# Two flamingo layers with a routed expert stage: one-hots of the routing in bf16 from a table of places, fewer filler matmuls ahead of the last turn, and another order of the last products

## The chip, the cores and the metric

One core of one Trainium2 chip. The time is that of the device in microseconds (us), from one launch of the whole program; lower is better. The engines are TensorE (PE; its weight loads are listed apart as PEld), VectorE (DVE), ScalarE (ACT), GpSimd (POOL) and the DMA queues, of which SyncE (SP) issues most.

## The reference

The input x is 2 x 1024 tokens of 256 values. Four stages add to it in turn:

```
x = x + tanh(g_xattn[0]) * L0_xattn(layernorm(x), ctx)   # one head, 77 keys
x = x + tanh(g_ffn[0])   * L0_ffn(layernorm(x))          # 256 -> 1024 -> 256, piecewise gelu on a grid
x = x + tanh(g_xattn[1]) * L1_xattn(layernorm(x), ctx)   # 16 heads, 77 keys
x = x + tanh(g_ffn[1])   * L1_ffn(layernorm(x))          # 8 experts, two choices per token
```

The last stage is the one that the change is about:

```
scores = softmax(xt @ wg)                 # 2048 tokens, 8 experts
gvals, gidx = top_k(scores, 2); gvals /= sum(gvals)
# for choice 0, then choice 1: pos = how many choices of this expert came before
keep = pos < 512                          # room of an expert
disp[expert, pos] = token                 # the tokens gathered by expert
y = gelu(disp @ w1 + b1) @ w2 + b2        # per expert
out[token] += gvals * keep * y[expert, pos]
```

## The kernel before, in words

The 2048 tokens lie in SBUF as 16 tiles of 128. All matmuls of float32 values are split into three (high by high, high by low, low by high part; `split_mm`, lines 1397 to 1402). Each engine has a program of its own, in which its order is written out by hand; engines wait for each other through semaphores. What the change touches lies in three places.

**The end of the second attention.** The tokens go through layer norm, a turn on TensorE and the routing logits in pieces (`PIECES`, line 27): three of four tiles, then two of two tiles. The last piece is round `round_of(3, 4)`. For it VectorE takes the statistics (`last_stats`, line 1229), GpSimd takes a power (`power`, line 577), VectorE scales the rows into `xn` (`apply`, line 951), TensorE turns them (`transpose_x`, line 1418), ScalarE copies the high part (`x_hi`, line 673), VectorE makes the low part (`x_lo`, line 959), and TensorE forms the logits (`logits_columns`, `logits_rows`). On VectorE stand between `apply` and `x_lo` of this piece: `take_logits(2)`, `take_logits(3)` and `top_two(3)` (lines 1175 to 1192). On TensorE stand in front of the turn the filler matmuls `keep_warm(5, 8)` (line 1444; 128 x 512 columns of ones each, whose results nobody reads), and behind it `keep_warm(5, 5)`.

**The routing.** With the two best experts of each token in `ixf` and their marks in `mask_bf`, three matmuls and a scan count the place of each choice within its expert (lines 1260 to 1264). A token's choice, one of 32 (`q`: 2 choices by 16 tiles) per partition, goes to slot 128 a + b, where a (0 to 31, `al`) is a tile of slots and b (0 to 127, `bl`) a row in it. `onehotA` (line 1284, float32) marks a, `onehotB` (line 1279, bf16, made in four parts by `rows_hot`) marks b. Both lie choice by choice, so the compare of one choice against the row `iota_a` or `iota_b` has the choice's own number repeated along the innermost dimension. ScalarE makes `sel_tok` from `onehotA`, multiplied by the partition's number plus one (line 892) and by the tile's number (line 895, 16 instructions). TensorE then sums 32 products of `onehotB[:, q, :]` (the stationary operand) and `sel_tok[:, q, :, :]` (line 1818), which gives each slot its token. VectorE turns that into indices (lines 1295 to 1301), GpSimd gathers the rows (line 636), and TensorE, after 16 fillers, turns the first of them. The gates of the slots follow in the experts' stage: `gate_selection` (line 1322) multiplies `onehotA` by three bf16 parts of the gates, and `gates_of_slots` (line 1826) takes 32 products of `onehotB` and `sel_gate`.

**The experts' stage and its end.** For 10 blocks of 4 pairs TensorE alternates `hidden` of one pair and `project` of the pair three before (`LAG`). The last block holds the tiles 2 and 3 of the last expert. `project` runs over tiles, six matmuls each, for one pair at a time. After tile 2 of the last pair it raises `half_done`, on which VectorE adds the bias (line 1352) and scales by the gate (line 1356), and GpSimd scatters the tile's 128 rows with an add (line 648). Tile 3 follows in the same way on `hT_used`; its sum lies in a PSUM bank of its own (`O_last`).

GpSimd's program in the region: the constants of the routing at lines 609 to 615, among them `iota_a` and `iota_b`, in the shadow of the attention; then low parts of weights (line 583) and powers; the last power (line 625) is followed by nothing until the gathers.

Of the kernel before, what the change touches and what calls it, by code (L numbers as in the profile page):

```python
# [14 lines left out]
P = 128  # L15
# [20 lines left out]
def flamingo_gated_two_layers(nc, x, ctx_512, g_xattn, g_ffn,  # L36
# [32 lines left out]
    with ExitStack() as ctx:  # L69
# [316 lines left out]
        def round_of(stage, c):  # L386
            return ROUNDS.index((stage, c))
# [154 lines left out]
        def _(pool):  # L542
# [68 lines left out]
            pool.iota(iota_a, pattern=[[P, 32]], base=0, channel_multiplier=0, **flag).then_inc(rt_consts, 1)  # L611
            pool.iota(iota_b, pattern=[[1, P]], base=0, channel_multiplier=0, **flag).then_inc(rt_consts, 1)
# [12 lines left out]
            power(round_of(3, 4))  # L625

# [35 lines left out]
        def _(act):  # L662
# [227 lines left out]
            act.wait_ge(rt_consts, 5)  # L890
# [25 lines left out]
        def _(dve):  # L916
# [260 lines left out]
            def top_two(c):  # L1177
# [11 lines left out]
                if c == 0:  # L1189
                    dve.wait_ge(rt_consts, 5)  # L1190
# [76 lines left out]
            mark(dve.tensor_scalar(expert_base, posk, float(CAP), 2.0 * NE * CAP, ALU.is_ge, ALU.mult))  # L1267
            link(dve.tensor_scalar(al.bitcast(I32), posk, 1.0 / P, -(0.5 - 0.5 / P), ALU.mult, ALU.add))
            link(dve.scalar_tensor_tensor(out=expert_base, in0=ixf.rearrange("p k t -> p (k t)"), scalar=float(CAP),
# [3 lines left out]
            link(dve.scalar_tensor_tensor(out=al, in0=al.bitcast(I32), scalar=float(P), in1=expert_base, op0=ALU.mult,  # L1273
                                          op1=ALU.add))
# [121 lines left out]
        def _(pe):  # L1396
# [438 lines left out]
            for G in range(NG + LAG):  # L1835
# [8 lines left out]
                if G >= LAG:  # L1844
                    project(NB_PAIRS + G - LAG)
# [25 lines left out]
```

## Time and profile before

| | us |
|---|---|
| median of 3 runs | 536.08 |
| lowest and highest | 533.62, 538.42 |
| the profiled execution | 534.69 |
| its span, first to last instruction | 533.0 |
| mean granted TensorE clock | 0.966 of full |

The profiled execution is 1.69 us longer than its span. A clock of 1.00 is 2.4 GHz, one of 0.50 is 1.2 GHz. Starts in the trace count from the start of the span. "Idle before" in brackets is the idle time of the engine ahead of the row, with what ended it; a row with "x4" merges four instructions.

### The profile page before, as it was taken

What the parts mean: (1) busy time and instruction counts of PE and PEld (TensorE: products, weight loads), DVE (VectorE), ACT (ScalarE), POOL (GpSimd) and SP (SyncE); (2) the same over time, 40 slices, a digit from 0 to 9 for tenths busy, and PEclk for the clock granted to TensorE, in tenths of its full rate; (3) what the DMA queues carried; (4) which work ended last, traced back from release to release, by engine and by line L of the source; (5) the groups of instructions that cost most, each with busy time, mean ns of one, the idle gap of its engine ahead of it and who ended that gap; (6) DMA issues with size and microseconds to landing.
All of it is one profiled execution on the core that took longest, in us unless ns stands there. A gap on an engine that the chain in (4) does not pass through costs nothing.

```text
span 533.0 us, 8648 instructions
## 1 busy us (share of the span) xinstructions
PE 489.5 (92%) x3268; PEld 414.4 (78%) x3268; DVE 397.5 (75%) x754; ACT 259.1 (49%) x408; POOL 146.6 (28%) x124
## 2 busy tenths in 40 slices
PE   7989889998899999899999838999999999999991
PEld 4777579797887777687777615998899999989991
DVE  4796999999998859859779786858575866757441
ACT  3665586766755545365655422335344344434120
POOL 4362100010001112013002204521434527273253
PEclk9999979999899999799999987999999999999996
DMA  7323000000000101220211531214446547372031
GB/s 227 123 50 121 0 2 0 1 1 0 2 1 2 41 1 41 79 80 24 96 41 41 179 98 50 71 20 120 126 94 182 112 133 153 119 156 56 4 42 18
DMA packets 37163, 36.07 MB, mean 68 GB/s; under 512 B 6456, under 2 KB 35970, under 8 KB 36994
## 3 DMA queue, kind: packets, MB, share of 16 engines
q1 hardware_dynamic: 30661, 27.65, 16.5%
q0 software_dynamic: 6144, 7.66, 8.5%
q8 instruction: 26, 0.43, 0.3%
q10 hardware_dynamic: 317, 0.21, 0.2%
q14 instruction: 15, 0.12, 0.1%
HBM read 27.70 MB, written 8.39 MB: 68 GB/s over the span
## 4 chain that ended last, share of the span: by engine, by line
PE 55%; DVE 27%; issue 7%; ACT 3%; SPq 2%; DMA 2%; POOL 1%; ACTq 0%; DVEq 0%; POOLq 0%
PE PS L1400 12%; PE PS L1401 12%; PE PS L1402 12%; PE PS L1775 5%; PE PS L1717 3%; DVE tmp L1084 3%; DVE tmp L1071 3%; PE PS L1642 3%; DVE hT_lo L1092 3%; PE PS L1418 2%; PE PS L1784 2%; SPq L515 2%; DVE st L935 2%; DVE xT_lo L959 2%; DVE tmp L1059 1%
## 5 line engine op out<-in xcount | busy, mean ns | idle before, releaser
L1400 PE MATMUL PS<-w_hi,hT_hi 128*128 128x256 f32 x384 | 112.2, 292 | 0.4 <-DVE hT_lo L1092 0.2
L1401 PE MATMUL PS<-w_lo,hT_hi 128*128 128x256 f32 x384 | 110.2, 287 | 0.0
L1402 PE MATMUL PS<-w_hi,hT_lo 128*128 128x256 f32 x384 | 110.0, 286 | 0.0
L907 ACT ACTIVATE tmp<-PS,biasT 128x512 f32<-128x512 f32 (+1 forms) x80 | 43.8, 599 | 111.6 <-PE PS L1402 111.6
L648 POOL DMA_INDIRECT out<-tmp,dst_idx x32 | 55.8, 1744 | 99.7 <-DVE tmp L1356 93.0
L1400 PE MATMUL PS<-xT_hi,w_hi 128*128 128x512 f32 (+1 forms) x224 | 81.2, 362 | 0.4 <-DVE xT_lo L959 0.4
L1401 PE MATMUL PS<-xT_lo,w_hi 128*128 128x512 f32 (+1 forms) x224 | 80.7, 360 | 0.0
L1402 PE MATMUL PS<-xT_hi,w_lo 128*128 128x512 f32 (+1 forms) x224 | 80.5, 359 | 0.0
L1400 PEld LDWEIGHTS PS<-w_hi,hT_hi 128*128 128x128 f32 x384 | 75.3, 196 | 3.8 <-issue 2.3
L1401 PEld LDWEIGHTS PS<-w_lo,hT_hi 128*128 128x128 f32 x384 | 75.3, 196 | 0.9
L1402 PEld LDWEIGHTS PS<-w_hi,hT_lo 128*128 128x128 f32 x384 | 75.1, 196 | 0.0
L1333 DVE CAST hT_hi<-tmp 128x1024 fp32r<-128x1024 f32 (+1 forms) x40 | 23.9, 597 | 63.3 <-ACT tmp L907 63.1
L583 POOL TENSOR_TENSOR w_lo<-w_raw,w_hi 128x512 fp32r<-128x512 f32 (+1 forms) x16 | 29.2, 1829 | 86.0 <-ACT w_hi L690 84.1
L1402 PEld LDWEIGHTS PS<-xT_hi,w_lo 128*128 128x128 f32 x224 | 42.4, 189 | 6.6
L1400 PEld LDWEIGHTS PS<-xT_hi,w_hi 128*128 128x128 f32 x224 | 42.5, 190 | 6.1 <-DVE xT_lo L959 0.9
L1401 PEld LDWEIGHTS PS<-xT_lo,w_hi 128*128 128x128 f32 x224 | 42.5, 190 | 5.5
L577 POOL TENSOR_TENSOR rstd<-ve,minus_half 128x4 f32<-128x4 f32 (+1 forms) x17 | 17.7, 1039 | 102.7 <-DVE ve L940 96.7
L636 POOL DMA_INDIRECT xn<-normed_rows,src_idx x32 | 36.1, 1128 | 28.4 <-DVE dst_idx L1301 18.9
L1775 PE MATMUL PS<-Vblk,tmp 128*128 128x136 f32 (+1 forms) x320 | 42.7, 281 | 0.0
L1335 DVE TENSOR_TENSOR hT_lo<-tmp,hT_hi 128x1024 fp32r<-128x1024 f32 (+1 forms) x40 | 40.6, 1015 | 1.4
L1775 PEld LDWEIGHTS PS<-Vblk,tmp 128*128 128x128 f32 (+1 forms) x320 | 39.6, 190 | 1.5 <-issue 0.8
L690 ACT ACTIVATE w_hi<-w_raw 128x1024 fp32r<-128x1024 f32 x36 | 38.1, 1057 | 4.3 <-DMA w_raw<-in_L_ffn_w 4.3
(235 smaller groups left out, 887.0 us busy)
## 6 DMA issues: line engine op xcount, KB each, us to landing
w_raw<-in_L_ffn_w SPq DMA_DIRECT2D x72, 256.0 KB, 3.2
residual<-in_x SPq DMA_DIRECT2D x4, 512.0 KB, 5.4
out<-residual SPq DMA_DIRECT2D x3, 512.0 KB, 3.8
normed_rows<-xn SPq DMA_DIRECT2D x3, 512.0 KB, 2.9
kv<-in_L_ffn_b SPq DMA_DIRECT2D x1, 1024.0 KB, 6.6
tmp<-in_L_xattn_Wq SPq DMA_DIRECT2D x2, 256.0 KB, 5.3
out<-residual SPq DMA_DIRECT2D x2, 256.0 KB, 4.2
normed_rows<-xn SPq DMA_DIRECT2D x2, 256.0 KB, 2.2
```

The source lines that it names most:

```text
L577: pool.tensor_tensor(rstd[:, r % NS, 0:n], ve[:, r % NS, 0:n], minus_half[:, 0:n], ALU.pow).then_inc(rstd_ready, 1)
L583: ins = pool.tensor_tensor(w_lo[:, u % RING, a:b, :, :].rearrange("p a b c -> p (a b c)"), w_raw[:, u % 2, a:b, :, :].rearrange("p a b c - ...
L636: pool.indirect_dma_start(xn[:, (NR + i) % 2, j, :], None, normed_rows, bass.IndirectOffsetOnAxis(ap=src_idx[:, a:a + 1].bitcast(U32), axi ...
L648: pool.indirect_dma_start(out_rows, bass.IndirectOffsetOnAxis(ap=dst_idx[:, a:a + 1].bitcast(U32), axis=0), yD[:, e % 2, j, :], None, boun ...
L690: act.activation(w_hi[:, u % RING, :, :, :].rearrange("p a b c -> p (a b c)"), w_raw[:, u % 2, :, :, :].rearrange("p a b c -> p (a b c)"), ...
L907: act.activation(gD[:, G % 2, f, 0:P * n], H[:, G % 2, f, 0:P * n], ACT.Gelu, bias=biasT[:, col:col + 1]).then_inc(e_gelu, 1)
L1333: dve.tensor_copy(hT_hi[:, k % 4, :, 0:n], gD[:, G % 2, :, 0:n]).then_inc(hhi_ready, 1)
L1335: dve.tensor_tensor(hT_lo[:, k % 4, :, 0:n], gD[:, G % 2, :, 0:n], hT_hi[:, k % 4, :, 0:n].bitcast(F32), ALU.subtract).then_inc(hlo_ready, 1)
L1400: pe.matmul(o, lh, rh, start=start, stop=False, skip_group_check=skip)
L1401: pe.matmul(o, lh, rl, start=False, stop=False, skip_group_check=skip)
L1402: return pe.matmul(o, ll, rh, start=False, stop=stop, skip_group_check=skip)
L1775: ins = pe.matmul(pv[:, m, :], eT[0:n, q, :], Vblk[0:n, j, 2 * b + m, :], start=(q == 0), stop=(q == 2 * KJ - 1), skip_group_check=True)
```

## The change

Four edits, in the places named above.

1. `iota_a` and `iota_b` go; a table `places` (bf16, 128 numbers by 32 choices, each number repeated over the choices) is made by one iota on GpSimd behind its last power. The choice is now the innermost dimension of `onehotA`, `onehotB`, `sel_tok`, `sel_gate` and `places`, and all of them are bf16.
2. The 16 instructions of line 895 on ScalarE go; VectorE makes that half of `sel_tok` with one product, between `onehotA` and `onehotB`. TensorE's products take their operands with a step of 32 elements.
3. `keep_warm(5, 8)` in front of the last turn becomes `keep_warm(5, 2)`.
4. At the end, tile 2 of the last two pairs comes first, then tile 3 of both.

```diff
-        iota_a = small_take(32)
-        iota_b = small_take(P // 2).bitcast(BF16)
+        al_b = small_take(16).bitcast(BF16)
+        tile_of = small_take(16).bitcast(BF16)
...
-        onehotB = view(6080, 2048).bitcast(BF16).rearrange("p (q n) -> p q n", q=32)
-        sel_tok = view(4096, 1024).bitcast(BF16).rearrange("p (q a n) -> p q a n", q=32, a=2)
-        sel_gate = view(2048, 1536).bitcast(BF16).rearrange("p (q a n) -> p q a n", q=32, a=3)
+        onehotB = view(6080, 2048).bitcast(BF16).rearrange("p (n q) -> p n q", q=32)
+        places = view(0, 2048).bitcast(BF16).rearrange("p (n q) -> p n q", q=32)
+        sel_tok = view(4096, 1024).bitcast(BF16).rearrange("p (v a q) -> p v a q", q=32, v=2)
+        sel_gate = view(2048, 1536).bitcast(BF16).rearrange("p (v a q) -> p v a q", q=32, v=3)
         spare = Vblk[:, :, :, :].rearrange("p j a n -> p (j a n)")
-        onehotA = spare[:, 0:1024].rearrange("p (q n) -> p q n", q=32)
+        onehotA = spare[:, 0:512].bitcast(BF16).rearrange("p (a q) -> p a q", q=32)
...
             power(round_of(3, 4))
+            pool.wait_ge(c_trA, 2 * NT)
+            pool.wait_ge(c_trB, NT)
+            pool.iota(places, pattern=[[1, P], [0, 32]], base=0, channel_multiplier=0, **flag).then_inc(rt_consts, 1)
...
-            act.activation(sel_tok[:, :, 0, :], onehotA, ACT.Copy, scale=part1)
-            for t in range(NT):
-                tiles = slice(t, t + NT + 1, NT)
-                ins = act.activation(sel_tok[:, tiles, 1, :], onehotA[:, tiles, :], ACT.Copy, scale=float(t))
-                if t % 4 == 3:
-                    ins.then_inc(rt_sel, 1)
+            act.activation(sel_tok[:, 0, :, :], onehotA, ACT.Copy, scale=part1).then_inc(rt_sel, 1)
...
-                here = slice(4 * part, 4 * part + 4)
-                dve.tensor_tensor(onehotB.rearrange("p (k t) n -> p k t n", k=2)[:, :, here, :],
-                                  bcast(bl.rearrange("p (k t) -> p k t", k=2)[:, :, here].unsqueeze(3), [P, 2, 4, P]),
-                                  bcast(iota_b.unsqueeze(1).unsqueeze(1), [P, 2, 4, P]),
+                here = slice(8 * part, 8 * part + 8)
+                dve.tensor_tensor(onehotB[:, :, here], bcast(bl[:, here].unsqueeze(1), [P, P, 8]), places[:, :, here],
                                   ALU.is_equal).then_inc(rt_hot, 1)
-            dve.tensor_tensor(onehotA, bcast(al.unsqueeze(2), [P, 32, 32]),
-                              bcast(iota_a.unsqueeze(1), [P, 32, 32]), ALU.is_equal).then_inc(rt_tile, 1)
+            dve.wait_ge(rt_consts, 5)
+            dve.tensor_tensor(onehotA, bcast(al_b.unsqueeze(1), [P, 32, 32]), places[:, 0:32, :],
+                              ALU.is_equal).then_inc(rt_tile, 1)
+            dve.wait_ge(rt_tile, 1)
+            dve.tensor_tensor(sel_tok[:, 1, :, :], onehotA, bcast(tile_of.unsqueeze(1), [P, 32, 32]),
+                              ALU.mult).then_inc(rt_sel, 1)
...
-                dve.tensor_tensor(sel_gate[:, :, a, :], onehotA,
-                                  bcast(gate_bf[:, a, :, :].rearrange("p k t -> p (k t)").unsqueeze(2),
+                dve.tensor_tensor(sel_gate[:, a, :, :], onehotA,
+                                  bcast(gate_bf[:, a, :, :].rearrange("p k t -> p (k t)").unsqueeze(1),
...
-            keep_warm(5, 8)
+            keep_warm(5, 2)
             transpose_x(round_of(3, 4))
...
-            for t in range(NT):
-                pe.wait_ge(rt_hot, t // 4 + 1)
-                pe.wait_ge(rt_sel, t // 4 + 1)
-                for q in (t, NT + t):
-                    ins = pe.matmul(PS[:, 4, 0:64], onehotB[:, q, :], sel_tok[:, q, :, :].rearrange("p a n -> p (a n)"),
-                                    start=(q == 0), stop=(q == 31))
+            pe.wait_ge(rt_sel, 2)
+            for q in range(32):
+                pe.wait_ge(rt_hot, q // 8 + 1)
+                ins = pe.matmul(PS[:, 4, 0:64], onehotB[:, :, q], sel_tok[:, :, :, q].rearrange("p v a -> p (v a)"),
+                                start=(q == 0), stop=(q == 31))
...
-                    ins = pe.matmul(slot_sums, onehotB[:, q, :],
-                                    sel_gate[:, q, :, :].rearrange("p a n -> p (a n)"),
+                    ins = pe.matmul(slot_sums, onehotB[:, :, q],
+                                    sel_gate[:, :, :, q].rearrange("p v a -> p (v a)"),
...
-                if G >= LAG:
+                if LAG <= G < NG + LAG - 2:
                     project(NB_PAIRS + G - LAG)
+            last = NB_PAIRS + NG - 1
+            project(last - 1, only=2)
+            project(last, only=2)
+            project(last - 1, only=3)
+            project(last, only=3)
```

The counts that the waits on `rt_consts` compare with follow edit 1 (5 becomes 4; `places` is the fifth, waited for ahead of `onehotA`). `al` and `expert_base` are now in tiles, not in rows, so that `al_b` fits bf16.

## Rows read from the trace of the kernel before

**Rows 1.** The page, part 1: busy time, share of the span, instructions.

```profile
PE 489.5 (92%) x3268; PEld 414.4 (78%) x3268; DVE 397.5 (75%) x754; ACT 259.1 (49%) x408; POOL 146.6 (28%) x124
```

**Rows 2.** The chain of waits, 292 to 350 us: start, us, what.

```profile
306.58 1.83 PE PS L1444 x8
308.41 0.45 PE PS L1418 x4
...
317.93 4.54 DVE tmp L1279 x4
...
326.43 2.79 DMA xn<-normed_rows,src_idx
```

**Rows 3.** The timeline, last piece of layer norm: start, us, engine, line, operation.

```profile
305.31 0.70 POOL L577 TENSOR_TENSOR rstd<-ve,minus_half 128x2 f32<-128x2 f32 x1 [5.60 <-DVE ve L1242]
306.04 0.73 DVE L951 TENSOR_SCALAR xn<-residual,mv,rstd 128x256 f32<-128x256 f32 x2 [0.81 <-POOL rstd L577]
...
307.87 0.31 DVE L1192 TENSOR_TENSOR tmp<-tmp 128x16 bf16<-128x16 f32 x2
309.58 0.69 DVE L959 TENSOR_TENSOR xT_lo<-PS,xT_hi 128x512 fp32r<-128x512 f32 x1 [1.40 <-ACT xT_hi L673]
```

**Rows 4.** The timeline, places where GpSimd and VectorE work at once, and an iota.

```profile
16.07 2.23 POOL L595 MEMSET Vblk<- 128x2560 f32 x1 [2.00 <-DVE xn L951]
17.77 0.55 DVE L940 TENSOR_SCALAR ve<-mv 128x4 f32<-128x4 f32 x1
...
170.94 0.24 POOL L612 IOTA tmp<- 128x128 bf16 x1
172.18 0.17 DVE L940 TENSOR_SCALAR ve<-mv 128x4 f32<-128x4 f32 x1
...
297.35 2.36 POOL L583 TENSOR_TENSOR w_lo<-w_raw,w_hi 128x1024 fp32r<-128x1024 f32 x1
298.91 1.27 DVE L951 TENSOR_SCALAR xn<-residual,mv,rstd 128x256 f32<-128x256 f32 x2
```

**Rows 5.** The timeline, the one-hots and the first products.

```profile
316.70 1.22 DVE L1284 TENSOR_TENSOR Vblk<-tmp 128x1024 f32<-128x1024 f32 x1
317.84 4.62 DVE L1279 TENSOR_TENSOR tmp<-tmp 128x1024 bf16<-128x1024 bf16 x4
318.02 1.15 ACT L892 ACTIVATE tmp<-Vblk,tmp 128x1024 bf16<-128x1024 f32 x1 [4.07 <-DVE Vblk L1284]
319.07 2.43 ACT L895 ACTIVATE tmp<-Vblk 128x64 bf16<-128x64 f32 x16
322.52 0.62 PE L1818 MATMUL PS<-tmp 128*128 128x64 bf16 x8 [0.52 <-DVE tmp L1279]
323.31 0.19 DVE L1295 COPY tmp<-PS 128x32 f32<-128x32 f32 x1
```

**Rows 6.** A group by line and form, VectorE: busy us, mean ns, idle before.

```profile
L1333 DVE CAST hT_hi<-tmp 128x1024 fp32r<-128x1024 f32 x24 | 16.9, 706 | 43.2 <-ACT tmp L907 43.2
```

**Rows 7.** The timeline, the products of the gates.

```profile
343.83 1.53 PE L1826 MATMUL PS<-tmp 128*128 128x96 bf16 x32 [0.46 <-DVE tmp L1322]
```

**Rows 8.** Windows: us, five engines' busy time, granted clock, DMA share, GB/s.

```profile
314.00:316.00 2.00, 0.01 (x1) 0.00 (x0) 1.84 (x5) 0.00 (x0) 0.00 (x0) 0.97 0.00 0
316.00:318.00 2.00, 0.00 (x0) 0.00 (x0) 1.90 (x7) 0.00 (x0) 0.00 (x0) 0.50 0.00 0
...
326.00:328.00 2.00, 2.00 (x10) 0.76 (x8) 1.74 (x8) 0.00 (x0) 1.39 (x3) 0.97 0.23 66
```

**Rows 9.** The chain of waits near the end, one matmul of many.

```profile
520.66 0.12 PE PS L1400
```

**Rows 10.** The timeline of the end: bias of tile 2, its scatter, the last scatter.

```profile
521.06 0.42 DVE L1352 TENSOR_TENSOR tmp<-PS,kv 128x256 f32<-128x256 f32 x1 [3.01 <-PE PS L1402]
...
522.65 1.56 POOL L648 DMA_INDIRECT out<-tmp,dst_idx  x1 [2.04 <-DVE tmp L1356]
524.52 1.57 POOL L648 DMA_INDIRECT out<-tmp,dst_idx  x1 [0.30 <-issue]
```

More of the change, by code:

```diff
@@ L610, in _ @@
             pool.iota(iota_e, pattern=[[1, NE]], base=0, channel_multiplier=0, **flag).then_inc(rt_consts, 1)
-            pool.iota(iota_a, pattern=[[P, 32]], base=0, channel_multiplier=0, **flag).then_inc(rt_consts, 1)
-            pool.iota(iota_b, pattern=[[1, P]], base=0, channel_multiplier=0, **flag).then_inc(rt_consts, 1)
+            pool.iota(tile_of, pattern=[[0, 2], [1, NT]], base=0, channel_multiplier=0, **flag).then_inc(rt_consts, 1)
             pool.iota(part1, pattern=[[1, 1]], base=1, channel_multiplier=1, **flag).then_inc(rt_consts, 1)
@@ L888, in _ @@
             act.activation(elog, elog, ACT.Exp).then_inc(rt_exp, 1)
[L890 removed]
+            act.wait_ge(rt_consts, 4)
             act.wait_ge(rt_tile, 1)
[L892 to L897 removed]
+            act.activation(sel_tok[:, 0, :, :], onehotA, ACT.Copy, scale=part1).then_inc(rt_sel, 1)
             x_hi(NR)
@@ L1189, in top_two @@
                 if c == 0:
-                    dve.wait_ge(rt_consts, 5)
+                    dve.wait_ge(rt_consts, 4)
                 for k in range(2):
@@ L1264, in _ @@
             link(dve.tensor_reduce(posk, maskf.rearrange("p e k t -> p (k t) e"), AX_X, ALU.add))
-            mark(dve.tensor_scalar(expert_base, posk, float(CAP), 2.0 * NE * CAP, ALU.is_ge, ALU.mult))
+            mark(dve.tensor_scalar(expert_base, posk, float(CAP), 2.0 * SLOT_TILES, ALU.is_ge, ALU.mult))
             link(dve.tensor_scalar(al.bitcast(I32), posk, 1.0 / P, -(0.5 - 0.5 / P), ALU.mult, ALU.add))
-            link(dve.scalar_tensor_tensor(out=expert_base, in0=ixf.rearrange("p k t -> p (k t)"), scalar=float(CAP),
+            link(dve.scalar_tensor_tensor(out=expert_base, in0=ixf.rearrange("p k t -> p (k t)"), scalar=float(CAP // P),
                                           in1=expert_base, op0=ALU.mult, op1=ALU.add))
@@ L1272, in _ @@
                                           op1=ALU.add))
[L1273 removed]
+            link(dve.scalar_tensor_tensor(out=al_b, in0=al.bitcast(I32), scalar=1.0, in1=expert_base, op0=ALU.mult,
                                           op1=ALU.add))
             def rows_hot(part):
[L1278 to L1281 removed]
+                here = slice(8 * part, 8 * part + 8)
+                dve.tensor_tensor(onehotB[:, :, here], bcast(bl[:, here].unsqueeze(1), [P, P, 8]), places[:, :, here],
                                   ALU.is_equal).then_inc(rt_hot, 1)
[L1284 to L1285 removed]
+            dve.wait_ge(rt_consts, 5)
[4 more added lines that the diff above has]
+                              ALU.mult).then_inc(rt_sel, 1)
             for q in range(4):
@@ L1587, in hidden, with project @@
                 ins.then_inc(hid_ready, 1)
-            def project(g):
+            def project(g, only=None):
                 u = unit_of(g)
@@ L1603, in project @@
                 alone = g >= NB_PAIRS + NG - PAIRS
-                for i in range(tile, tile + count):
+                for i in range(tile, tile + count) if only is None else [only]:
                     for f in range(2):
@@ L1614, in project @@
                         ins.then_inc(half_done, 1)
-                ins.then_inc(hT_used, 1)
+                if only != 2:
+                    ins.then_inc(hT_used, 1)
             def queries_of(c):
```

## The prediction

> **What bounds the kernel now.** I read the page's busy shares first. The reader is to see that TensorE is busy 92% of the span and VectorE 75% [rows 1], so nearly everywhere an edit on VectorE or ScalarE is worth nothing. Next I read the chain of waits between 292 and 350 us, because it tells where TensorE is not the bound. It runs through the eight fillers, the last turn, VectorE's four parts of `onehotB` and then the gather of the first rows [rows 2]; from 331 us on it is TensorE's matmuls one after the other, up to the last scatters. So the stretch from 306 to 331 us is serial: a microsecond won or lost in it shifts all that follows. The timeline of this stretch gives the terms [rows 3, 5], the clock's windows what TensorE's clock did in it [rows 8]. The experts' stage counts only where TensorE stands idle, and the one such place that the change touches is in front of the products of the gates [rows 7]. At the end the last two scatters follow each other on GpSimd [rows 10].
>
> **Edit 3, the fillers.** Eight fillers take 1.83 us and the last turn's matmuls start behind them, at 308.41 [rows 2]. The rows to be turned are ready long before: `apply` ends at 306.04 + 0.73 = 306.77 [rows 3]. A filler of 512 columns at 2.4 GHz takes 512 / 2.4 = 213 ns (eight with the first one's start 1.83 us), so six fewer give 6 x 0.213 = 1.28 us, and two fillers end at 307.1, still behind 306.77. VectorE is free for `x_lo` at 307.87 + 0.31 = 308.18, and it would be wanted at 309.58 - 1.28 = 308.30 [rows 3], so nothing else is in the way. By itself the edit gives -1.28 us.
>
> **Edit 1, the table.** This edit puts an iota of 128 x 4096 elements right behind GpSimd's power, which ends at 306.01 [rows 3]. The trace has an iota of 128 elements in 0.24 us, and a memset of 2560 in 2.23 us, or 0.87 ns an element [rows 4]; by the latter it takes 4096 x 0.87 = 3.55 us. (The small iota with its start in it gives more than that per element; below, I see no row that would make it shorter than half.) It ends at about 309.55, and VectorE needs the table at 316 us or later, so the wait for it costs nothing. What it does to VectorE while it runs is another matter. During GpSimd's memset, which ends at 18.30, a VectorE `tensor_scalar` of four elements began at 17.77 and ended at 18.32; the same instruction with GpSimd still takes 0.17 us [rows 4]. Two `tensor_scalar` of `apply` that began at 298.91 under GpSimd's product (end 299.71) took 1.27 us, against 0.73 us for the same two at 306.04, and the second ended 0.47 us behind GpSimd's end [rows 3, 4]. So such an instruction of VectorE waits until GpSimd's is over. In the changed kernel the `apply` of the last piece starts at 306.04 and the iota at about 306.0, both released by the same power. I take it that the iota comes first. Then `xn` is ready at 309.55 + 0.47 = 310.02, in place of 306.77. On VectorE `take_logits` and `top_two(3)` follow; they end 308.18 - 306.77 = 1.41 us after `apply` [rows 3], at 311.43. The turn, the high part and the handing over take 309.58 - 308.41 = 1.17 us [rows 2, 3], which with 0.1 us for the start gives 311.3. `x_lo` then starts at 311.43 in place of 309.58: +1.85 us, and in this case the fillers' -1.28 is not had at all, since TensorE waits for `xn` anyhow. If VectorE gets both its instructions in first, the cast of `top_two(3)` at 307.7 meets the iota instead, and the loss is about 1.3 us; the bounds of this term are thus -1.28 (the iota disturbs nothing) and +1.85, and a little more if the iota is slower than the memset. I take +1.85, by the memset's row.
>
> The Trainium skill, "SBUF — State Buffer", section "Who interferes with whom", says that VectorE in a two-port mode (which `tensor_scalar` and casts can enter) and GpSimd hold a shared pair of ports for a whole instruction, whoever comes first, and that this holds for a GpSimd instruction that only writes. By that rule the iota does block, and the sum is the one with +1.85; the trace agrees for the memset, and has no case of an iota beside such an instruction.
>
> **Edits 1 and 2 on VectorE.** Before, `onehotA` starts at 316.70 and the last part of `onehotB` ends at 317.84 + 4.62 = 322.46, that is 5.76 us [rows 5]; one 128 x 1024 product takes 1.22 us alone and follows the one before after 1.135 us. No row shows a two-operand instruction with both operands bf16 and contiguous. The bounds are the present 1.135 us between starts (at float32 1.22 us for one, as at bf16) and the pace of a contiguous one-operand cast of the same 1024 elements, 706 ns [rows 6]. I take the cast's pace, because what the present bf16 compares lack against the new ones is just the contiguous innermost run: 0.69 us alone, 0.60 us between starts. Then: `onehotA` 0.69, a handing over of 0.02, `sel_tok`'s second half 0.60, four parts 4 x 0.60 + 0.09: 3.80 us, or 5.76 - 3.80 = 1.96 us less. ScalarE's remaining copy of 1.15 us [rows 5] starts 0.1 us behind `onehotA` and ends about when the first part does; its 16 small ones ended at 321.50, ahead of VectorE, so leaving them out gives nothing more. The last eight products then take 0.62 us behind the last part [rows 5], and VectorE itself has 0.85 us of other work there, as before. So -1.96 us, with +1.25 as the other bound: at the old pace the one product more costs 1.14 us, and the handing over the rest.
>
> The Trainium skill, "VectorE: DVE Perf Modes", section "The perf-mode tier table", gives `tensor_tensor` in bf16 twice the rate of float32 when the innermost step is one. By that rule the sum is the one taken; the present bf16 compares, with a step of zero on one operand, run at the float32 pace, which the trace shows [rows 5].
>
> **Steps on TensorE.** The products now read both operands with a step of 64 bytes. No row has such an operand. Below, they cost what they do now, 1.53 / 32 = 48 ns for each product of the gates at full clock, and 0.62 / 8 = 77 ns for each of the slots [rows 5, 7] at half clock: the clock stands at 0.50 (1.2 GHz) from 316 us, after 2 us with next to nothing on TensorE (busy 0.01 us from 314 on), and is back at full over nearly all of 326 to 328, after some 6 us of products and fillers [rows 8]. Above, I take twice as much. For the slots I take nothing, since at half clock the array itself takes columns at half the rate and leaves the reads twice the time. For the gates, at full clock, I take the middle, +0.77 us (bounds 0 and +1.53). They stand in the experts' stage on TensorE itself, so all of it counts.
>
> **The gates' wait.** TensorE now stands 0.46 us in front of the gates' products for the third `gate_selection` [rows 7]. Each of the three takes about as long as a compare of 1024, and at the new pace the third comes 3 x 0.53 us earlier: the wait goes, -0.46 us. At the old pace it stays.
>
> **Edit 4, the end.** Six matmuls of one tile and pair at 0.12 us [rows 9] are 0.72 us. `half_done` comes that much earlier, since tile 3 of the pair before now stands behind it. VectorE's bias at 521.06, the scatter at 522.65 and the one at 524.52 follow each other [rows 10] and move by 0.72. Tile 3's sum is complete when it was, and scaled at about 522.6, ahead of the last scatter's new start at 523.8. The operands of the last pair's product were split long before. -0.72 us, not less than 0 and not more.
>
> **Elsewhere.** The two small iotas that go and the one that comes stand at 171 us with TensorE busy: 0. The 16 fillers behind the slots' products start when these end and move with them, as the gather does.
>
> **The sum**, against the profiled execution of 534.69 us: +1.85 - 1.96 + 0.77 - 0.46 - 0.72 = -0.52, so 534.2. The median of the runs shown is 1.39 us above the profiled one; I give 535.6 us. A measurement of this kernel tells about 1% (5 us) from no change, so this is no change.
>
> **The rivals.**
> *The iota disturbs nobody* (chance 0.2). Then the fillers' gain is had: -1.28 - 1.96 + 0.77 - 0.46 - 0.72 = -3.65, or 532.4 us. For it: no row has an iota beside a `tensor_scalar`. Against it: the memset, which also only writes, holds it up.
> *Stepped operands slow TensorE* (0.17), the case on the slower side. Each product takes twice as long, 96 ns in the gates and 154 ns in the slots. The slots' products then no longer hide behind VectorE: the first part is ready at 316.70 + 1.85 + 2.0 = 320.6, 32 x 0.154 = 4.9 us later it is 325.5, in place of 323.14, so +2.4 stands for +1.85 - 1.96. With +1.53 - 0.46 - 0.72 it is +2.75: 538.8 us. It decides from about 40 ns more per product of the gates, which eats up the -1.29 of the other terms. For it: every read lies 64 bytes from the last, in both operands; against it: nothing in the trace.
> The Trainium skill, "SBUF — State Buffer", section "Specifications (TRN2)", has lines of 16 bytes that want two hits each for full bandwidth, which a step of 64 bytes never gives; it names no price, and by it this rival holds.
> *The bf16 instructions keep the old pace* (0.05), so that the change does not do what it says: +1.85 + 1.25 + 0.77 - 0.72 = +3.15, the gates' wait stays: 539.2 us.
> *The clock falls in front of the last turn* (0.08): with `xn` late, TensorE idles from 307.1 to 310.0, longer than the 2 us after which it fell at 316 [rows 8]. At half clock five fillers take 2.1 us in place of 1.07, and the logits' matmuls about 0.4 us more: +1.4 on the forecast, 537.0 us.
> The forecast has 0.5.
>
> **The range.** It takes in the first rival with stepped operands at no cost (-4.42, 531.7 us) and the second at its price (538.8): 531.5 to 538.8, and leaves out about 2 in 10. Faster by over 1% needs that first case and a lucky run: 0.08. Slower by over 1% needs two of the dear cases together: 0.07. Within 1%: 0.85.
>
> **What would show it.** The iota: 3.5 us from 306.0, and `apply` of the last piece ending near 310 and not at 306.8; if it ends at 306.8 and no cast behind it is long, the first rival holds. VectorE: compares of 0.69 us and 3.8 us from `onehotA` to the end of `onehotB`. Products: 48 ns apart in the gates, 77 in the slots, or more. No idle in front of the gates' products. The last two scatters 0.72 us earlier against TensorE's last matmul. A time outside 531.5 to 538.8 would make the forecast wrong, and so would a front stretch that gains where I have it lose.

## The result, and the profile after

| kernel | runs | median us | profiled execution us | its span us | granted clock |
|---|---|---|---|---|---|
| before | 4 | 537.25 | 534.69 | 533.0 | 0.966 |
| after | 4 | 544.94 | 541.53 | 539.8 | 0.961 |

After takes 1.0184 times as long as before, 95% interval 1.0129 to 1.0239: slower by over 1%. Some executions of either kernel fall into a slower state (before's 542.53 us); here and below the medians are of all executions and the ratios of the others alone, so a ratio is not the quotient of two medians. The prediction said no change, 535.6 us in a range of 531.5 to 538.8; the median lies 6.1 us above that range.

The two profiled executions can't be laid on each other by their absolute times: the last power of the layer norm starts at 305.31 us before and at 302.39 us after. The 2.92 us between them arise between 215 and 242 us, where no edit is. TensorE's granted clock tells them apart: 0.54 from 220 to 224 us and 0.61 from 224 to 228 before, and 1.00 in both after, though TensorE had been busy for 2.23 of the 4 us ahead in either. Of the eleven profiled executions of the full kernel in this document three had that fall (before, its repeat and moving2), and in these three alone the power starts at 305 us or later. So everything below is counted from the start of that power. Counted so, the last scatter comes 219.21 us after it before and 228.98 us after it in the changed kernel: 9.77 us more, of which the repeats below show a part to be that execution's own.

The timeline of the last piece of layer norm, after (columns as in [rows 3], to which it answers):

```profile
302.39 0.69 POOL L578 TENSOR_TENSOR rstd<-ve,minus_half 128x2 f32<-128x2 f32 x1 [5.60 <-DVE ve L1240]
303.05 4.17 POOL L628 IOTA tmp<- 128x4096 bf16 x1
303.12 4.56 DVE L949 TENSOR_SCALAR xn<-residual,mv,rstd 128x256 f32<-128x256 f32 x2 [0.81 <-POOL rstd L578]
307.74 1.12 PE L1419 MATMUL PS<-ident,xn 128*128 128x128 f32 x4 [3.53 <-DVE xn L949]
308.64 2.15 PE L1445 MATMUL PS<-ones_bf 128*128 128x512 bf16 x5
309.59 0.69 DVE L957 TENSOR_TENSOR xT_lo<-PS,xT_hi 128x512 fp32r<-128x512 f32 x1 [0.49 <-ACT xT_hi L676]
```

The two `tensor_scalar` of `apply` began 0.07 us after the iota and took 4.56 us in place of 0.73, ending 0.46 us behind the iota's end. TensorE stood 3.53 us for `xn`, and its clock fell while it stood, as these windows of after show (us, busy time of PE, PEld, DVE, ACT, POOL, granted clock, DMA share, GB/s):

```profile
304.00:306.00 2.00, 0.21 (x1) 0.00 (x0) 2.00 (x1) 0.00 (x0) 2.00 (x1) 1.00 0.00 0
306.00:308.00 2.00, 0.26 (x1) 0.27 (x2) 1.97 (x6) 0.00 (x0) 1.22 (x1) 0.76 0.00 0
308.00:310.00 2.00, 2.00 (x8) 1.11 (x8) 1.41 (x10) 0.60 (x1) 0.00 (x0) 0.50 0.63 192
```

Five fillers took 2.15 us, and 1.24 us before. The timeline of the one-hots and the first products, after, answers to [rows 5]:

```profile
317.32 0.69 DVE L1281 TENSOR_TENSOR Vblk<-tmp 128x1024 bf16<-128x1024 bf16 x1
318.04 0.69 DVE L1284 TENSOR_TENSOR tmp<-Vblk,tmp 128x1024 bf16<-128x1024 bf16 x1
318.65 2.49 DVE L1277 TENSOR_TENSOR tmp<-tmp 128x1024 bf16<-128x1024 bf16 x4
319.48 4.10 PE L1819 MATMUL PS<-tmp 128*128 128x64 bf16 x32 [4.86 <-DVE tmp L1277]
323.69 0.19 DVE L1295 COPY tmp<-PS 128x32 f32<-128x32 f32 x1 [1.73 <-PE PS L1819]
```

VectorE does what was forecast: the last part of `onehotB` ends at 318.65 + 2.49 = 321.14, 3.82 us after `onehotA` began (forecast 3.80, before 5.76). But the 32 products of the slots take 4.10 us, 128 ns each where it was 77, and VectorE now stands idle for 1.73 us waiting for them, where before it stood for nothing. The chain of waits says the same: its piece in this place was `onehotB` on VectorE [rows 2], and after it is TensorE (start, us, what):

```profile
319.48 4.11 PE PS L1819 x32
```

The products of the gates, timeline of after, which answer to [rows 7]:

```profile
345.50 5.83 PE L1827 MATMUL PS<-tmp 128*128 128x96 bf16 x32 [1.64 <-DVE tmp L1322]
```

They take 5.83 us in place of 1.53, 182 ns each in place of 48. The windows of after with the instructions of that line alone (us, PE, PEld, granted clock, DMA share, GB/s), and in a second fence later windows with all instructions (columns as before):

```profile
346.00:348.00 2.00, 2.00 (x14) 1.67 (x13) 1.00 0.00 0
348.00:350.00 2.00, 2.00 (x13) 1.69 (x12) 0.50 0.00 0
```

```profile
352.00:354.00 2.00, 2.00 (x12) 2.00 (x11) 0.00 (x0) 0.00 (x0) 0.00 (x0) 0.50 0.00 0
```

Look at the counts: the products pass at the same pace, 14 and 13 in 2 us, at granted clock 1.00 and at 0.50. What holds them does not follow the clock. And the clock falls under them although TensorE is busy without a gap by the records, and is still at 0.50 from 352 to 354, so that the experts' matmuls behind them step by 0.21 us in place of 0.12.

The end, timeline of after, answers to [rows 10]:

```profile
529.51 1.55 POOL L651 DMA_INDIRECT out<-tmp,dst_idx  x1 [1.32 <-DVE tmp L1357]
```

GpSimd waits 1.32 us ahead of the scatter of tile 2, and 2.04 before: 0.72 less, as forecast.

The difference by sections, in us, for the profiled executions and for a repeated execution of either kernel (below):

| section | before | after | change | change, repeats |
|---|---|---|---|---|
| last power to `onehotA` | 11.39 | 14.93 | +3.54 | +4.07 |
| `onehotA` to the copy of the slots' sums | 6.61 | 6.37 | -0.24 | -0.22 |
| to the first expert's first matmul | 7.87 | 7.93 | +0.06 | -0.02 |
| to the gates' products | 12.65 | 13.88 | +1.23 | -0.59 |
| the gates' products | 1.53 | 5.83 | +4.30 | +4.29 |
| from these to the last scatter | 179.16 | 180.04 | +0.88 | +1.17 |
| sum | | | +9.77 | +8.70 |

The profiled times themselves differ by 6.84 us only, since before lost the 2.92 us ahead of the power.

### The profile page after: what moved, and what is told of

It reads as the page before. It is cut to its first block, busy times and chain, and to the rows that moved or that the text cites. A ratio compares the mean times of both kernels' runs of the same rounds, so it can differ in the third digit from the quotient of the medians.

```text
span 539.8 us, 8608 instructions
## 1 busy us (share of the span) xinstructions
PE 492.2 (91%) x3262; PEld 417.6 (77%) x3262; DVE 398.2 (74%) x755; ACT 256.6 (48%) x392; POOL 149.8 (28%) x124
## 4 chain that ended last, share of the span: by engine, by line
PE 54%; DVE 28%; issue 8%; ACT 3%; SPq 2%; POOL 2%; DMA 2%; another core or an unknown queue 0%; DVEq 0%; ACTq 0%; POOLq 0%
PE PS L1401 12%; PE PS L1402 12%; PE PS L1403 12%; PE PS L1777 5%; DVE tmp L1082 3%; DVE tmp L1069 3%; PE PS L1719 3%; DVE hT_lo L1090 3%; PE PS L1644 3%; DVE st L933 2%; PE PS L1786 2%; PE PS L1419 2%; DVE xn L949 2%; SPq L516 2%; DVE xT_lo L957 1%
```

## The experiments

Two theories stood after the comparison. A: the step between the elements that TensorE reads sets the pace of its products; it eats up the one-hots' gain and costs over 4 us at the gates, and the iota adds its hold on `apply`. B: something else in the new stage makes the products slow (the clock, or the stationary operand's step).

**The price of a step by itself.** `step_prices` leaves the whole computation out but for copying `x` to the output, and runs chains of 24 products at full clock, with stationary and moving operand laid out at steps of 1 to 32 elements of bf16:

```diff
+            def W(s, q):
+                return w[:, 0:P * s].rearrange("p (n q) -> p n q", q=s)[:, :, q % s]
+            def M(s, q, n=96):
+                return m[:, 0:n * s].rearrange("p (n q) -> p n q", q=s)[:, :, q % s]
...
+            for q in range(24):
+                pe.matmul(PS[:, 1, 0:96], W(32, q), M(1, q, 96), start=True, stop=True)
```

> Leaves out the whole computation except a copy of x: twelve groups of 24 bf16 products (128x128 stationary) with 22 fillers of 512 columns after each. The groups differ in the step, in elements of 2 bytes, of the stationary and of the moving operand. In the changed kernel a product of 96 columns with both steps at 32 takes 5.83/32 = 182 ns, one of 64 columns 4.11/32 = 128 ns, against 48 ns with both at 1. Theory A (the moving operand's reads set the pace, by columns): 1/1 48 ns, 32/1 about 50 ns, 1/32 about 180 ns, 32/32 about 180 ns, 64 columns 125 ns. Rival B (the weight load sets it): 32/1 about 180 ns and 1/32 about 50 ns; but then 64 and 96 columns should cost the same. Steps 16 and 8 (32 and 16 bytes) as 32, step 4 (8 bytes) between, step 2 (4 bytes) near 48 to 60 ns, if what counts is how many reads fall into one piece of memory.

The chain of waits of step_prices (start, us, what; steps of stationary/moving operand, in the order of the lines: 1/1, 32/1, 1/32, 32/32, 8/8, 4/4, 2/2, then 32/32 with 64 columns, 4/1, 1/4; left out are 16/16 with 4.38 us and 1/1 with 64 columns with 0.70):

```profile
20.52 1.02 PE PS L57 x24
26.29 1.47 PE PS L60 x24
32.51 3.92 PE PS L63 x24
41.18 4.24 PE PS L66 x24
...
62.40 4.26 PE PS L72 x24
72.74 2.15 PE PS L75 x24
79.64 1.04 PE PS L78 x24
85.43 2.95 PE PS L81 x24
...
98.58 1.02 PE PS L87 x24
104.35 2.08 PE PS L90 x24
```

The moving operand alone at step 32 takes the product from 1.02 / 24 = 43 ns to 163 ns; the stationary one alone only to 61 ns; both give 177 ns, near the 182 ns of the gates. With 64 columns both give 123 ns, near the 128 ns of the slots. With both operands stepped, a column costs about 1.8 ns from a step of 8 elements (16 bytes) on, half of that at 4 elements (8 bytes), and no more than packed at 2 (4 bytes). The steps of 8, 16 and 32 elements on both operands thus cost about the same. So theory A has its price, and the surprise is in it that the step of 64 bytes is no worse than one of 16; the stationary operand's 61 ns lie above the 50 expected.

One thing more stands in this trace. Behind each chain follow 22 fillers. From the same chain of waits:

```profile
66.67 5.64 PE PS L44 x20
...
74.89 4.75 PE PS L44 x22
```

The first row stands behind the chain 8/8, where 20 fillers took 5.64 us; the second behind 4/4, where all 22 took 4.75. Behind 32/32 and 16/16 it is as behind 8/8: the granted clock stood at 0.50 from 46 to 48, from 56 to 58 and from 66 to 68 us, and at 1.00 behind the other nine chains. So such a slow stretch follows stepped products also where no other engine computes; it did not follow the chain 1/32, whose products are stepped too and took 3.92 us.

**The iota alone.** Before, with only the large iota and a wait for it:

```diff
+            pool.wait_ge(c_trA, 2 * NT)
+            pool.wait_ge(c_trB, NT)
+            pool.iota(places, pattern=[[1, P], [0, 32]], base=0, channel_multiplier=0, **flag).then_inc(rt_consts, 1)
...
+            dve.wait_ge(rt_consts, 6)
```

> The kernel before with only the iota of 128x4096 at the place it has in the changed kernel; nothing reads it. Theory (it holds up the scaling of the last piece): iota 4.2 us, the two scalings 4.5 us in place of 0.73, the front of the routing 1.9 to 3 us later, time +2 to +3.5 us. Rival (the late xn of the changed kernel has another cause, such as the fillers): no change of the time, scalings 0.73 us.

Measured: 539.34 us, ratio 1.0117 (1.0054 to 1.018). Timeline of iota_alone:

```profile
302.88 4.18 POOL L629 IOTA tmp<- 128x4096 bf16 x1
302.95 4.57 DVE L955 TENSOR_SCALAR xn<-residual,mv,rstd 128x256 f32<-128x256 f32 x2 [0.81 <-POOL rstd L578]
317.17 1.23 DVE L1289 TENSOR_TENSOR Vblk<-tmp 128x1024 f32<-128x1024 f32 x1
```

`onehotA` starts 14.95 us after the last power (302.22), as in after, and not 11.39: the whole +3.54 of the first row of the table is the iota's, and it hides the fillers' saving wholly. It is settled that the iota holds `apply` up. The time rose by more than the 2 to 3.5 us expected: the ratio is worth 2.9 to 9.6 us, and the trace has 5.71 from the last power to the last scatter, 1.77 of them in the first expert, where ScalarE has waits of 1.41 and 2.21 us of the kind that is told of under the repeats.

**The table without the iota.** After, with the table spread by ScalarE in four copies of 1024 from a small one, so that GpSimd has nothing beside `apply`:

```diff
-            pool.iota(places, pattern=[[1, P], [0, 32]], base=0, channel_multiplier=0, **flag).then_inc(rt_consts, 1)
...
+                act.activation(places[:, here, :], bcast(iota_b[:, here].unsqueeze(2), [P, 32, 32]),
+                               ACT.Copy).then_inc(rt_table, 1)
```

> The changed kernel with the table made by ScalarE in four copies of 1024 from a row of 128 numbers, in place of GpSimd's iota. Theory: scalings back to 0.73 us; onehotA starts 3.5 us or more earlier against the power of the last piece; fillers' gain had; 4 to 5 us faster than the changed kernel. Rival (the iota costs little in the end since the slots' products take the loss up): under 2 us faster.

Measured: 539.41 us, ratio 1.0058 (1.0013 to 1.0104). Timeline of act_table:

```profile
303.18 0.74 DVE L961 TENSOR_SCALAR xn<-residual,mv,rstd 128x256 f32<-128x256 f32 x2 [0.81 <-POOL rstd L580]
...
312.57 0.69 DVE L1293 TENSOR_TENSOR Vblk<-tmp 128x1024 bf16<-128x1024 bf16 x1
...
318.96 0.19 DVE L1307 COPY tmp<-PS 128x32 f32<-128x32 f32 x1 [1.74 <-PE PS L1831]
...
343.51 5.83 PE L1839 MATMUL PS<-tmp 128*128 128x96 bf16 x32
```

`onehotA` comes 312.57 - 302.45 = 10.12 us after the power, 4.8 us earlier than in after, while both sets of products cost what they did (VectorE waits 1.74 us for the slots', the gates' take 5.83). Even without the iota the change is slower than before, by 0.6% with an interval that ends just above 1. This execution has a stall of 2.45 us of TensorE in the first expert; see the repeats.

**Fillers and end alone.** Before, with edits 3 and 4 and nothing of the one-hots:

```diff
-            keep_warm(5, 8)
+            keep_warm(5, 2)
...
+            project(last - 1, only=2)
+            project(last, only=2)
+            project(last - 1, only=3)
+            project(last, only=3)
```

> The kernel before with only the fillers (8 to 2) and the order of the last products changed; the routing as before. Theory: -1.3 and -0.7, so 2 us faster than before, with both seen in the trace. Rival (fewer fillers lower the clock in the last turn and logits): the 1.3 are lost, matmuls of the logits at 0.23 us in place of 0.12.

Measured: 531.57 us, ratio 0.9946 (0.9916 to 0.9976). Timeline of fill_end:

```profile
305.47 0.69 DVE L959 TENSOR_TENSOR xT_lo<-PS,xT_hi 128x512 fp32r<-128x512 f32 x1
...
341.18 1.53 PE L1827 MATMUL PS<-tmp 128*128 128x96 bf16 x32 [1.03 <-DVE tmp L1322]
```

`x_lo` starts 2.99 us after the power (302.48), and 4.27 before: -1.28 to the hundredth, and the clock doesn't fall. From the end of the gates' products to the last scatter it takes 178.43 us in place of 179.16: -0.73, edit 4's share. Against these 178.43, after's 180.04 holds 1.61 us more. The clock behind its stepped products accounts for them: between 351.40 and 354.81 us TensorE made sixteen steps of 0.21 us, which at 0.12 us each would be 1.5 us less.

**The moving operand's step alone, in the whole kernel.** After, with the tile one-hots and both selections in groups of two choices (a moving column 4 bytes from the next); the iota and the stationary step of 64 bytes stay:

```diff
-        sel_gate = view(2048, 1536).bitcast(BF16).rearrange("p (v a q) -> p v a q", q=32, v=3)
+        sel_gate = view(2048, 1536).bitcast(BF16).rearrange("p (g v a r) -> p g v a r", g=16, v=3, r=2)
...
-                    ins = pe.matmul(slot_sums, onehotB[:, :, q],
-                                    sel_gate[:, :, :, q].rearrange("p v a -> p (v a)"),
+                    ins = pe.matmul(slot_sums, onehotB[:, :, q],
+                                    sel_gate[:, q // 2, :, :, q % 2].rearrange("p v a -> p (v a)"),
```

> The kernel after, with one thing laid out anew: the tile one-hots and what is made of them (the moving operands of the slots' and the gates' products) lie in groups of two choices, so that a moving column is 4 bytes from the next and not 64; the stationary one-hots keep their step of 64 bytes, and the iota behind the last power stays. Theory A (step_prices: the moving operand's step sets the pace, the stationary one's costs little; 32/1 took 61 ns and 2/2 43 ns per 96 columns): the 32 gates' products take about 32 x 61 = 1.95 us at full clock (after 5.83, before 1.53), the 32 slots' products no longer outlast VectorE's one-hots, so that they end with the last of these (before the copy of the sums VectorE waits under 0.5 us, after 1.73), and TensorE's clock stays up or comes back earlier in the stretch of the gates' products; ratio to before about 1.018 - (3.9 + 1.5 + 1.5)/537 = 1.005. Theory B (the step of the stationary operand is what costs in the whole kernel): the gates' products stay near 180 ns each and the ratio near 1.018. Open beside both: VectorE's compares with only two choices innermost may lose the doubled pace (0.69 us for 1024 elements with it, about 1.2 us without).

Measured: 535.58 us, ratio 1.0006 (0.9972 to 1.004), a little better than Theory A's 1.005. Timeline of moving2:

```profile
320.91 1.01 DVE L1285 TENSOR_TENSOR Vblk<-tmp 128x1024 bf16<-128x1024 bf16 x1
...
323.41 2.44 PE L1821 MATMUL PS<-tmp 128*128 128x64 bf16 x32 [5.18 <-DVE tmp L1277]
...
325.95 0.19 DVE L1298 COPY tmp<-PS 128x32 f32<-128x32 f32 x1
...
346.73 2.24 PE L1829 MATMUL PS<-tmp 128*128 128x96 bf16 x32 [0.66 <-DVE tmp L1325]
```

and a window of it (columns as above):

```profile
348.00:350.00 2.00, 2.00 (x26) 2.00 (x25) 0.14 (x1) 0.00 (x0) 0.00 (x0) 1.00 0.04 8
```

The gates' products take 70 ns in place of 182 (61 were expected), the slots' 76 in place of 128 and end with VectorE's last part, the wait of 1.73 us is gone, and the clock stands at 1.00 from 346 to 352, through and behind the gates' products. From these to the last scatter it is 178.46 us, fill_end's number. Theory B falls: the stationary operand still has its 64 bytes here. One thing is dearer: the compare of `onehotA` took 1.01 us, and its table is read there as pairs 64 bytes apart; in grouped (next), where the pairs lie 8 bytes apart, it takes 0.69.

**The change without its costs.** `grouped` has the row one-hots in groups of four choices, the tile one-hots in groups of two, and a table of only 128 x 4 elements, made at 171 us among the old iotas; edits 3 and 4 stay. `grouped_only` is the same without edits 3 and 4, `grouped4` has groups of four for both:

```diff
-            pool.iota(places, pattern=[[1, P], [0, 32]], base=0, channel_multiplier=0, **flag).then_inc(rt_consts, 1)
+            pool.iota(places[:, :, :], pattern=[[1, P], [0, RB]], base=0, channel_multiplier=0, **flag).then_inc(rt_consts, 1)
...
+        RB, RA = 4, 2
+        onehotB = view(6080, 2048).bitcast(BF16).rearrange("p (g n r) -> p g n r", g=32 // RB, r=RB)
...
+                dve.tensor_tensor(onehotB[:, here, :, :], bcast(bl.rearrange("p (g r) -> p g r", r=RB)[:, here, :].unsqueeze(2), [P, g, P, RB]),
+                                  bcast(places[:, :, :].unsqueeze(1), [P, g, P, RB]), ALU.is_equal).then_inc(rt_hot, 1)
```

> The whole change with the costs taken out: row one-hots in groups of four choices (a stationary column 8 bytes from the next), tile one-hots in groups of two, the table only 128 x 4 elements and made by GpSimd at the old iotas' place (about 171 us), so that nothing runs on GpSimd beside the apply of the last piece; fewer fillers and the end in the new order as in the change. Theory A: the start of the one-hots relative to the last power is as in fill_end (10.12 us), VectorE's one-hots end 3.8 us later and the copy of the slots' sums follows within 0.5 us, gates' products take 1.4 to 1.95 us for all 32; against before -1.28 (fillers) -1.96 (one-hots) -0.46 (gate selections) -0.72 (end) = -4.4 us, ratio 0.992 (fill_end alone 0.9946). Theory B (any step of an operand costs, or the short innermost run of two or four choices takes VectorE's pace back): the one-hots take as long as before (5.8 us) or the products outlast them, and the ratio is fill_end's 0.9946 or above it.

> The kernel before with the one-hots of grouped alone (old number of fillers, old order at the end). Theory A: start of the one-hots 11.39 us after the last power as before, then 1.96 us less until the copy of the slots' sums and 0.46 us less at the gates: 2.4 us less than before, ratio about 0.9955. Theory B: no gain, ratio 1.000. A third possibility, the clock: if a later half-speed stretch appears in the last turn or the gates' products, the gain goes there (about 1.5 us).

> grouped, but with the tile one-hots too in groups of four choices (a moving column 8 bytes from the next): step_prices gave 90 ns per 96 columns for this step against 43. The 32 gates' products take about 2.9 us (grouped 1.4 to 1.95), the slots' products about 32 x 60 ns = 1.9 us, still within VectorE's 2.5 us, so only the gates' side shows it: about 1 us above grouped. If groups of two take VectorE's doubled pace away and groups of four don't, the compare of the tile one-hots is 0.69 us here and above 0.69 in grouped, and grouped4 may come out ahead.

| kernel | median us | ratio | 95% interval | gates' 32 products |
|---|---|---|---|---|
| grouped | 529.06 | 0.9864 | 0.981 to 0.9918 | 1.65 us |
| grouped_only | 530.24 | 0.9898 | 0.9832 to 0.9965 | 1.63 us |
| grouped4 | 530.09 | 0.9903 | 0.987 to 0.9936 | 3.06 us |

Timeline of grouped:

```profile
170.96 1.20 POOL L614 IOTA places<- 128x512 bf16 x1
...
312.46 0.69 DVE L1283 TENSOR_TENSOR Vblk<-tmp,places 128x1024 bf16<-128x1024 bf16 x1
313.79 2.49 DVE L1277 TENSOR_TENSOR tmp<-tmp,places 128x1024 bf16<-128x1024 bf16 x4
...
317.13 0.19 DVE L1296 COPY tmp<-PS 128x32 f32<-128x32 f32 x1
```

The doubled pace of VectorE holds with runs of only two and four elements innermost (0.69 us), and from `onehotA` to the copy it takes 4.67 us in place of 6.61: the 1.94 us that edits 1 and 2 were to bring, had in full. In grouped_only the section sums are 11.42, 4.68, 7.90 and 12.21 us against before's 11.39, 6.61, 7.87 and 12.65, so -2.31 by the trace, as forecast (-2.4). From the gates' products to the last scatter it takes 179.18 us in grouped_only and 178.42 in grouped: edit 4's share once more. All three run faster than before; their intervals overlap, so that the traces and not the times say what each part is worth. The ratios of grouped and grouped_only are also better than the 0.992 and 0.9955 expected. Part of that is not the edits': counted from the last power to the last scatter, grouped is 2.55 us faster than before (with a wait of 2.86 us of ScalarE in it, see the repeats), while the profiled executions differ by 5.5. The other 2.96 us are the fall of the clock between 220 and 228 us that before's execution had and grouped's had not. How often either kernel meets it, and so how much of the ratios it makes up, is not known. grouped4's gates cost 1.4 us more than grouped's, as the price of 8 bytes foretold.

**The repeats.** In the first expert, between its first matmul and the gates' products, the profiles lie between 12.1 and 16.1 us; after's +1.23 is within that. ScalarE waited 2.9 us there on what the profile calls remote. Either kernel was run and profiled once more, unchanged:

> A second look at the kernel after, unchanged: is the later start of the gates' products relative to the first expert's first matmul (13.88 us against 12.65 before, with ScalarE waiting up to 2.9 us on something the profile calls remote) the kernel's or one execution's? If it belongs to the change (more steps in flight, other programs), it comes again at 13.9 with the same wait at the same place. If it is scatter between executions, as the 12.1 to 16.1 us of the nine profiles so far suggest, it comes out elsewhere in that span, while the gates' products themselves take 5.8 us again and the one-hots start 14.9 us after the last power again.

> A second look at the kernel before, unchanged. Scatter: the last power lies at about 302.4 or at about 305.3 us (both places have been seen, and the stretch between 215 and 242 us in which they part is edited in no kernel), the one-hots start 11.4 us after it as before, and from the first expert's first matmul to the gates' products it takes something between 12.1 and 14.5 us rather than 12.65 exactly. If instead the places are the kernels' own, this one shows 305.3 and 12.65 again.

Measured: 541.12 us (after) and 536.15 us (before), one execution each. Timeline of after_again, then of before_again:

```profile
303.40 4.56 DVE L949 TENSOR_SCALAR xn<-residual,mv,rstd 128x256 f32<-128x256 f32 x2 [0.81 <-POOL rstd L578]
318.47 0.69 DVE L1281 TENSOR_TENSOR Vblk<-tmp 128x1024 bf16<-128x1024 bf16 x1
```

```profile
345.26 1.53 PE L1826 MATMUL PS<-tmp 128*128 128x96 bf16 x32 [0.46 <-DVE tmp L1322]
```

The remote wait did not come again: in after_again that section takes 12.06 us, 0.59 less than before's 12.65, which before_again repeats exactly. So after's +1.23 was that execution's and not the change's, and under it lies the gain forecast for the gates' wait. What the wait is stays open; one of over 1 us was seen in four of the profiles (after, iota_alone, act_table, grouped), and nothing was tried on it. It is not all of the scatter: fill_end has 14.03 us in this section without it. The start of the one-hots came 15.80 us after the power, 0.87 later than expected: the clock stood at 0.50 through 308 to 314 us here, and in the first profile it was back at 0.88 from 310 on. before_again's one-hots start 11.73 us after its power, 0.34 later than before's: its clock stood at 0.50 from 314 to 316 us, and before's at 0.97. Its last power lies at 306.35, outside both places expected. That no edit sets this place shows in moving2 (305.52) and iota_alone (302.22).

## Why the prediction was wrong

The step that failed is "Steps on TensorE": it put the price of the stepped operands at +0.77 us in all (0 for the slots, +0.77 for the gates), and the runs showed +1.7 at the slots, +4.30 at the gates and +1.61 by the clock behind them. Beside it the iota's term was mis-sized. Point by point, by the terms of the sum:

- **The iota holds up `apply`, +1.85: right in mechanism, too small in size.** It took 4.17 us, against 3.55 by the memset's pace. `apply` ended 0.46 us behind it, as the rows had it, and the order on VectorE was the one forecast. But the term was +3.54, and +4.07 in the repeats. 0.62 of the missing 1.69 is the iota's length; the rest fits the falling clock, which the prediction had as a rival with 0.08 and +1.4 us: the last turn took 1.12 us in place of 0.60, and from the start of `x_lo` to `onehotA` it took 7.73 us in place of 7.12. No run held the clock up beside the iota, so this split is read from the trace and not shown by an experiment. That rival should have been part of the forecast: the prediction's own rows had the clock fall behind a stretch in which TensorE did next to nothing [rows 8], and its own sum had TensorE wait for `xn`.
- **Edits 1 and 2 on VectorE, -1.96: right on VectorE, and not had.** 3.82 us where 3.80 was forecast. The copy of the slots' sums comes 1.94 us earlier behind `onehotA` in grouped, and 0.24 us in after, because the slots' products outlast VectorE.
- **Slots' products, 0: wrong.** The argument was that at half clock the reads have twice the time. They need about as long at either clock, 2.0 ns per column at half (4.10 us / 32 / 64 columns) and 1.9 at full (123 ns / 64 in step_prices), against 1.2 ns that half clock gives them (77 ns / 64). The bound of twice as much was there, 154 ns, and 128 was measured; what was wrong was to take its lower end for a reason that no row bore out.
- **Gates' products, +0.77: wrong by 3.5 us.** 182 ns each, where the upper bound was 96. This is the largest error, and it lies outside the bounds: "twice" stood for an unknown, with no row behind it. The rival of the stepped operands, 0.17, named the mechanism that held, and had the price of the gates at a third of the excess it was (1.53 of 4.30).
- **Behind the gates' products: not in the prediction.** The clock falls under stepped products, 1.61 us. The prediction put this at nothing and gave no reason.
- **The gates' wait, -0.46: right.** -0.59 in the repeats, with no idle time of TensorE ahead of these products; the first execution hides it under a wait of its own.
- **Edit 4, -0.72: right,** -0.73 in fill_end. **Edit 3, -1.28 by itself: right** to the hundredth in fill_end, and hidden in after by the iota, as the prediction said.

With the measured sizes in the places of the terms, the sum is +3.54 - 0.24 + 0.06 - 0.59 + 4.30 + 1.61 - 0.73 = +7.95 us (the section of the first expert from the repeats). From the last power on the executions say 9.77 and 8.70; the medians say 7.7, the ratio 9.9 with an interval from 6.9 to 12.8. Two of the dear cases came together here, the falling clock and the stepped operands, for which the prediction had 0.07.

The rule quoted from the Trainium skill, "SBUF — State Buffer", section "Who interferes with whom", held for the iota: VectorE's `tensor_scalar` waited until it ended. The Trainium skill's rule on lines of 16 bytes, "SBUF — State Buffer", section "Specifications (TRN2)", named the right rival. It also says that two hits in a line give full bandwidth; by it a step of 8 bytes would be free, and step_prices has 2.08 us for 24 products with it against 1.02 without. The measurement decides. The rule of the Trainium skill, "VectorE: DVE Perf Modes", section "The perf-mode tier table", held too, at 0.69 us for 1024 elements against 1.22.

Edits 3 and 4 were worth having, and the one-hots' new layout was worth it only for the engine that writes them. Who wants both has `grouped`: 0.9864 of before, and by the medians 529.06 against 534.74 us.

## What to carry to other kernels

When a layout is changed for the engine that writes it, price the engine that reads it as well, first in a chain of two dozen instructions on the chip: the one that gained 1.9 us here was not the one that paid 6. A group of two or four elements innermost served both here: VectorE kept its doubled pace on runs of two, and TensorE read steps of 4 bytes for next to nothing (1.04 us for 24 products against 1.02). A table that an engine makes late should be small or early: 512 elements at 171 us cost nothing, and 4096 beside the critical `tensor_scalar` cost 3.5 us. And compare stretches of a trace from a common event near the edit: here three executions of eleven had lost about 3 us to the clock before any edit came into play.

## What the runs showed of the hardware that was not expected

- Per column of a bf16 product: 1.8 to 1.9 ns with both operands at a step of 16, 32 or 64 bytes, 1.7 with the moving one alone at 64, 0.9 with it alone at 8, and no more than packed (43 ns for 96 columns) with both at 4. A stationary operand costs nothing at 8 bytes and 18 ns per 128 columns at 64.
- The pace of stepped products was the same at granted clock 1.00 and 0.50, 14 and 13 products in 2 us.
- TensorE's granted clock fell to 0.50 during 32 such products in a row with no gap in its records, and stayed there for some 7 us; it stood at 1.00 in moving2, with 70 ns per product. In step_prices it fell at the end of the chains 32/32, 16/16 and 8/8, and behind no other.
- In a stretch that no edit touches the clock fell in three of eleven profiled executions (0.51 to 0.73 from 220 to 224 us) and stood at 1.00 in the other eight; the first three start the last power about 3 us later.
- GpSimd's iota took 4.17 us for 4096 elements of bf16, 1.20 us for 512 in runs of four, and 0.24 us for 128 [rows 4]: neither a fixed price per element nor one fit by the memset's.
